# A recommendation tower on one Trainium2 core: the low half of a split product two operations behind, a tenth split step in every fourth unit, one tile turned later

## The chip, the cores and the metric

The kernel runs on one core of one Trainium2 chip. The metric is the device time of one launch in microseconds, the median of several runs. Five engines work side by side: TensorE (PE in the rows; its weight loads are PEld), VectorE (DVE), ScalarE (ACT), GpSimd (POOL) and SyncE (SP), which only issues transfers. They meet through semaphores.

## The reference

For each of 2048 rows, 39 embedding vectors of 16 numbers are looked up in 39 tables: `e[b, f, d]`. Two layers of crossed products follow, then a small dense tower:

```
z0 = einsum('bid,bjd->bdij', e, e)           # 39*39 products per (b, d)
cur0 = relu(z0 @ W0)                         # 128 channels
next_h, direct0 = split(cur0, 2)             # 64 go on, 64 go out
z1 = einsum('bid,bjd->bdij', e, next_h)      # 39*64 products per (b, d)
cur1 = relu(z1 @ W1)                         # 128 channels
z = sum over d of [direct0, cur1]            # 192 features
h = [z, dense_ctx]; two relu layers (512, 256) and a row of weights give y
```

Everything is in 32-bit floats. The time goes into the two einsums with their weights.

## The kernel before

**Tiles and units.** The batch is cut into 16 tiles of 128 rows, and each tile into two halves of the 16 embedding columns. That makes 32 units, numbered 0 to 31, of 1024 columns each (8 embedding columns times 128 rows). In a unit the products of one step stand on 128 partitions by 1024 columns, and the weights of the step (128 by 128) contract the partitions. The second layer has 20 steps in a unit, s0 to s19 (`step1`); s12 is a step on half the columns. The first layer of unit u+1 has 6 or 7 steps, here called a0 to a6 (`step0`), which are woven into unit u behind the steps named in `AFTER`. So a1 follows s1, a4 follows s7 and a5 follows s9.

**Whole and split steps.** VectorE multiplies two operands into a buffer (`make`, L965). A whole step goes into one of seven buffers `z`, and TensorE multiplies it in 32-bit floats (`product`, L561; each of its two matmuls shows as two records). A split step goes into one of three buffers `z_split`. ScalarE copies it to `z_hi` in the shorter type fp32r (`high`, L831), VectorE subtracts that from the product to get `z_lo` (`low`, L974), and TensorE makes three pairs of matmuls: `z_hi` with the high weights (L591), `z_hi` with the low weights (L594), `z_lo` with the high weights (L598, behind a wait on `z_lo_made`). In a unit the steps a1, a4 and s2, s3, s7, s8, s9, s13, s14 are split, nine in all, so VectorE has two operations for each of these and one for the others. In program order they stand in runs: a1, s2, s3, then s7, a4, s8, s9, then s13, s14.

**Who waits for what.** `make` of split number n waits until `z_lo` of split n-3 is made, since the `z_split` buffer is used again (L961). `high` of split n waits until TensorE has used split n-3 (L830). Each engine runs its instructions strictly in the order written. In what order VectorE makes its products and its `z_lo` is set by `low_before`, which is called behind each product; `place` is the number of a step in that order.

**Turning a tile.** GpSimd gathers the embedding rows of a tile (39 indirect DMAs, fewer for the first two tiles), TensorE transposes them (`turn_tile`, L553) at the step that `turn_step` names, ScalarE copies them out (`keep_tile`, L763 and L764) two steps later and issues four DMAs that store them (`store_tile`, L376), and SyncE loads the operands of the next tile's units from there. ScalarE stands in one row of work with this: in `body` the `keep_tile` comes ahead of the `high` of the same step. At the end of a unit ScalarE makes the operands of the next one from the first layer's result (`relu0`).

Of the kernel before, what the change touches and what calls it, by code (L numbers as in the profile page):

```python
# [35 lines left out]
STEPS1 = 2 + 2 * FQ  # L36
LAYS = 1 + FQ
SPLIT0 = (1, 4)
HALF1 = 12
SPLIT1 = (2, 3, 7, 8, 9, 13, 14)  # L40
WHOLE0 = tuple(s for s in range(STEPS0) if s not in SPLIT0)
REST0 = 3
EARLY = (2, 3)
WHOLE1 = tuple(s for s in range(STEPS1) if s not in SPLIT1 or s in EARLY)
ORDER0 = SPLIT0 + WHOLE0
AFTER = (0, 1, 3, 5, 7, 9, 11)
AHEAD = 2
# [51 lines left out]
def turn_step(u):  # L99

    if u % 2 or u + 2 >= UNITS:
        return None
    return {0: 11, 2: 7}.get(u, 2)


def lay_parts(n):
# [30 lines left out]
def at1(u, s):  # L137

    return FIRST1[u] + s + sum(a < s for a in after(u))
# [14 lines left out]

def split1(u):

    return tuple(s for s in SPLIT1 if u > 0 or s not in EARLY)


SPLIT_AT = sorted([at0(u, s) for u in range(UNITS) for s in split0(u)] + [at1(u, s) for u in range(UNITS) for s in split1(u)])  # L160
WHOLE_AT = sorted([at0(u, s) for u in range(UNITS) for s in range(steps0(u)) if s not in split0(u)] +
                  [at1(u, s) for u in range(UNITS) for s in range(STEPS1) if s not in split1(u)])
WHOLE_NO = {place: n for n, place in enumerate(WHOLE_AT)}
LEFT_AT = {at0(u, STEPS0 - 1): u for u in range(UNITS) if left_units(u)}
HALF_AT = {at1(u, HALF1) for u in range(UNITS)}
SPLIT_NO = {place: n for n, place in enumerate(SPLIT_AT)}


def shape_of(place):

    if place in LEFT_AT:
        return left_rows(LEFT_AT[place]), BANK
    return P, BANK if place in HALF_AT else C


def tower(nc, ids, tables, hot_ids, hot_tables, hot_consts, ident_in, dense_t, w0_a, w0_b, w1_whole, w1_split, top, top_small, y):
    ctx = ExitStack()
    with ctx:
        def sb(name, shape, dt=FP):
            return ctx.enter_context(nc.sbuf_tensor(name, shape, dt))  # L180
# [31 lines left out]
        w0_lo = sb("w0_lo", [P, len(SPLIT0), L], FR)  # L212
        w1 = sb("w1", [P, len(WHOLE1), L])
        w1_hi = sb("w1_hi", [P, len(SPLIT1), L], FR)
        w1_lo = sb("w1_lo", [P, len(SPLIT1), L], FR)
        small = sb("small", [P, K1 + K2 + K2])
# [22 lines left out]
        def half(t, u):  # L239
            return t[:, (u % 2) * C:(u % 2 + 1) * C]  # L240
# [30 lines left out]
        w0_raw_b = r0[:, C:C + STEPS0 * L].rearrange("p (s l) -> p s l", s=STEPS0)  # L271
        w1_raw = r1[:, 0:len(SPLIT1) * L].rearrange("p (s l) -> p s l", s=len(SPLIT1))

# [269 lines left out]
        def _(pe):  # L543
# [12 lines left out]
            def product(ps, place, k, w, first, last):  # L556

                pe.wait_ge(z_made, place + 1)
                for c in range(C // BANK):
                    cs = slice(c * BANK, (c + 1) * BANK)  # L560
                    mm = nc.tensor.matmul(ps[:, cs], w[0:k, :], z[WHOLE_NO[place] % NZ][0:k, cs], start=first, stop=last)  # L561
                mm.then_inc(z_used, 1)

            def half_product(ps, place, w, last):

                pe.wait_ge(z_made, place + 1)
                for n in range(2):
                    rows = slice(n * HROWS, (n + 1) * HROWS)
                    mm = nc.tensor.matmul(ps[:, n * BANK:(n + 1) * BANK], w[rows, :],  # L569
                                          z[WHOLE_NO[place] % NZ][rows, 0:BANK], start=False, stop=last)  # L570
                mm.then_inc(z_used, 1)
# [13 lines left out]
            def split_product(ps, place, k, w_hi, w_lo, first, last):  # L585

                n = SPLIT_NO[place]
                pe.wait_ge(z_hi_made, n + 1)
                for c in range(C // BANK):
                    cs = slice(c * BANK, (c + 1) * BANK)  # L590
                    nc.tensor.matmul(ps[:, cs], w_hi[0:k, :], z_hi[n % NS][0:k, cs], start=first, stop=False)  # L591
                for c in range(C // BANK):
                    cs = slice(c * BANK, (c + 1) * BANK)
                    nc.tensor.matmul(ps[:, cs], w_lo[0:k, :], z_hi[n % NS][0:k, cs], start=False, stop=False)  # L594
                pe.wait_ge(z_lo_made, n + 1)
                for c in range(C // BANK):
                    cs = slice(c * BANK, (c + 1) * BANK)
                    mm = nc.tensor.matmul(ps[:, cs], w_hi[0:k, :], z_lo[n % NS][0:k, cs], start=False, stop=last)  # L598
                mm.then_inc(z_used, 1)
# [14 lines left out]
            def step1(u, s):  # L614
                if s == 0 and u >= 2:
                    pe.wait_ge(relu1_done, u - 1)
                if s == HALF1:
                    half_product(half(psB, u), at1(u, s), w1[:, WHOLE1.index(s), :], False)
                elif s in split1(u):
                    n = SPLIT1.index(s)  # L620
                    split_product(half(psB, u), at1(u, s), P, w1_hi[:, n, :], w1_lo[:, n, :], s == 0, s == STEPS1 - 1)
                else:
                    product(half(psB, u), at1(u, s), P, w1[:, WHOLE1.index(s), :], s == 0, s == STEPS1 - 1)

# [57 lines left out]
            for u in range(UNITS):  # L682
                for s in range(STEPS1):
                    if s == turn_step(u):
                        turn_tile(u // 2 + 1)
                    step1(u, s)
                    if s in after(u):
                        step0(u + 1, after(u).index(s))
# [67 lines left out]
        def _(act):  # L756
# [76 lines left out]
            def body(u):  # L833
                for s in range(STEPS1):
                    if turn_step(u) is not None and s == turn_step(u) + 2:
                        keep_tile(u // 2 + 1)
                    if s in split1(u):
                        high(at1(u, s))
                    if s in after(u) and after(u).index(s) in split0(u + 1):
                        high(at0(u + 1, after(u).index(s)))  # L840
                    if s == REST0 and u == 0:
                        relu0_rest(0)
                    if s == 6 and u >= 1:
                        relu1(u - 1)
                    if s == 7 and u == UNITS - 1:
                        act.wait_ge(top_loaded, 32)
                        nc.scalar.activation(w_top_hi[:, 0:2 * C], w_top[0], ACT.Copy).then_inc(top_hi_made, 1)
                        nc.scalar.activation(w_top_hi[:, 2 * C:], w_top[1], ACT.Copy).then_inc(top_hi_made, 1)
                if u + 1 < UNITS:
                    relu0(u + 1)  # L850
# [101 lines left out]
        def _(dve):  # L952
# [14 lines left out]
            def low(place):  # L967

                k, cols = shape_of(place)
                n = SPLIT_NO[place]  # L970
                dve.wait_ge(z_hi_made, n + 1)
                if n >= NS:
                    dve.wait_ge(z_used, SPLIT_AT[n - NS] + 1)
                nc.vector.tensor_tensor(z_lo[n % NS][0:k, 0:cols], z_split[n % NS][0:k, 0:cols], z_hi[n % NS][0:k, 0:cols].bitcast(FP),  # L974
                                        ALU.subtract).then_inc(z_lo_made, 1)
# [47 lines left out]
                    relu_copy(h_quad[0][k][j * QUAD:(j + 1) * QUAD, BANK:C], rows, quad_copied)  # L1023

            def low_before(place):
                if place - 1 in SPLIT_NO:
                    low(place - 1)

            def sum0(q):
                dve.wait_ge(relu0_done, 4 * q + 4)  # L1030
# [27 lines left out]
            def body(u):  # L1058
                for s in range(STEPS1):
                    step1(u, s)  # L1060
                    if s == 17 and u == UNITS - 1:
                        split_top()
                    low_before(at1(u, s))
                    if u == 0 and s == 0:
                        copy_quad(0)
                    if s in after(u):
                        step0(u + 1, after(u).index(s))
                        low_before(at0(u + 1, after(u).index(s)))
                    if u == 0 and s == 1:
                        copy_quad(1)  # L1070
                    if s == 15 and u == 0:
                        dense_low()
                    if s == STEPS1 - 2 and u % 2 == 0 and u >= 2:
                        sum1(u // 2 - 1)
                    if s == STEPS1 - 2 and u % 4 == 3 and u < UNITS - 1:
                        sum0(u // 4)
# [119 lines left out]
            for s in range(STEPS0):  # L1196
                step0(0, s)
                low_before(at0(0, s))
# [144 lines left out]
```

## Time and profile before

| | |
|---|---|
| median of 3 runs | 1447.1 us (1446.37 to 1447.96) |
| the profiled execution | 1451.1 us, its span 1448.1 us |
| mean granted TensorE clock | 0.993 |
| TensorE busy | 1417.3 us (98% of the span) |
| VectorE busy | 1380.9 us (95%) |
| ScalarE busy | 783.7 us (54%) |
| GpSimd busy | 993.9 us (69%) |

The times in the trace count from the start of the span. The first products of unit 0 begin at 40.9 us, the steps of unit 31 end at about 1398 us, and the rest is the dense tower. A row of the timeline gives the start, the duration, the engine, the line, the operation with the tiles it writes and reads, and how many instructions are merged in it; in brackets stands the idle time ahead of it and who ended it. The time from one instruction's start to the next one's on the same engine tells what it costs there; durations overlap a little.

### The profile page before, as it was taken

The numbers are of one execution on the slowest core, as the hardware profiler recorded it, in microseconds if no ns is written. First come the engines' busy times: TensorE is split into PE (matmuls) and PEld (weight loads), VectorE is DVE, ScalarE is ACT, GpSimd is POOL, SyncE is SP. The second block draws the span as 40 slices with busy tenths as digits, with TensorE's granted clock in tenths as the row PEclk, the third lists the DMA queues.
The fourth block names the chain that finished last, engine by engine and source line by source line (L and its number), as shares of the span: only waits on it lengthen the run. The fifth ranks groups of instructions, "written<-read, shape, count | busy, mean of one in ns | idle before, by whom it ended". The sixth has DMA issues, their size and how long they took to land.

```text
span 1448.1 us, 14670 instructions
## 1 busy us (share of the span) xinstructions
PE 1417.3 (98%) x4408; PEld 783.3 (54%) x4408; DVE 1380.9 (95%) x1243; ACT 783.7 (54%) x833; POOL 993.9 (69%) x604
## 2 busy tenths in 40 slices
PE   4999999999999999999999999999999999999999
PEld 3545554555555555555555555555555555555556
DVE  6899999999999999999999999999999999999983
ACT  1555446555455656545465565545656554565655
POOL 7888888888888888888888888888888840000000
PEclk7999999999999999999999999999999999999999
DMA  5979788788888888878788887888898877777600
GB/s 156 212 190 236 185 223 200 196 219 201 203 210 200 215 205 217 213 197 216 205 200 211 213 225 190 205 210 206 203 224 212 211 201 198 201 200 208 180 13 0
DMA packets 130779, 282.64 MB, mean 195 GB/s; under 512 B 36532, under 2 KB 61764, under 8 KB 130572
## 3 DMA queue, kind: packets, MB, share of 16 engines
q1 hardware_dynamic: 96588, 268.31, 70.6%
q0 software_dynamic: 19200, 4.95, 4.1%
q10 hardware_dynamic: 14912, 8.46, 2.0%
q8 instruction: 34, 0.56, 0.2%
q14 instruction: 45, 0.37, 0.1%
HBM read 273.67 MB, written 7.87 MB: 194 GB/s over the span
## 4 chain that ended last, share of the span: by engine, by line
PE 81%; POOL 13%; issue 3%; DVE 1%; DMA 1%; ACT 0%; DVEq 0%; POOLq 0%
PE psB L561 39%; POOL emb L538 13%; PE psA L561 13%; PE psB L591 6%; PE psB L594 6%; PE psB L598 6%; PE psB L569 2%; PE psA L591 2%; PE psA L594 2%; PE psA L598 2%; PE psA L581 1%; PE psB L693 1%; PE psA L553 1%; PE psB L695 1%; PE psB L694 1%
## 5 line engine op out<-in xcount | busy, mean ns | idle before, releaser
L538 POOL DMA_INDIRECT emb<-in_tbl,ids_all x600 | 993.7, 1656 | 185.0 <-issue 182.6
L561 PE MATMUL psB<-z,w 128*128 128x512 f32 x1544 | 689.3, 592 | 2.6 <-DVE z L965 2.6
L831 ACT ACTIVATE z_hi<-z_split 128x1024 fp32r<-128x1024 f32 x285 | 301.0, 1060 | 512.2 <-DVE z_split L965 447.2
L561 PEld LDWEIGHTS psB<-z,w 128*128 128x128 f32 x1544 | 292.7, 190 | 358.2 <-issue 333.5
L965 DVE TENSOR_TENSOR z<-h_quad,x_lay 128x1024 f32<-128x1024 f32 x354 | 419.0, 1213 | 2.0 <-issue 1.3
L974 DVE TENSOR_TENSOR z_lo<-z_split,z_hi 128x1024 fp32r<-128x1024 f32 x285 | 348.9, 1224 | 21.0 <-ACT z_hi L831 20.9
L965 DVE TENSOR_TENSOR z_split<-h_quad,x_lay 128x1024 f32<-128x1024 f32 x222 | 266.6, 1213 | 0.0
L785 ACT ACTIVATE h_quad<-psA 32x1024 f32<-32x1024 f32 x248 | 251.8, 1015 | 6.7 <-DVE feat_side L1056 3.1
L561 PE MATMUL psA<-z,w 128*128 128x512 f32 x516 | 242.2, 592 | 0.5 <-DVE z L965 0.5
L591 PE MATMUL psB<-z_hi,w_hi 128*128 128x512 f32 x444 | 155.9, 432 | 0.0
L561 PEld LDWEIGHTS psA<-z,w 128*128 128x128 f32 x516 | 97.4, 189 | 99.5 <-issue 91.0
L598 PE MATMUL psB<-z_lo,w_hi 128*128 128x512 f32 x444 | 138.6, 393 | 1.7 <-DVE z_lo L974 1.6
L594 PE MATMUL psB<-z_hi,w_lo 128*128 128x512 f32 x444 | 138.6, 394 | 0.0
L965 DVE TENSOR_TENSOR z<-bases,x_more 128x1024 f32<-128x1024 f32 x93 | 112.7, 1212 | 0.4 <-DMA x_more<-x_tiles 0.4
L591 PEld LDWEIGHTS psB<-z_hi,w_hi 128*128 128x128 f32 x444 | 80.1, 189 | 52.1 <-issue 37.6
L598 PEld LDWEIGHTS psB<-z_lo,w_hi 128*128 128x128 f32 x444 | 82.8, 189 | 23.5 <-DVE z_lo L974 5.8
L594 PEld LDWEIGHTS psB<-z_hi,w_lo 128*128 128x128 f32 x444 | 83.7, 188 | 18.7
L777 ACT ACTIVATE h_pair<-psA 64x1024 f32<-64x1024 f32 x62 | 62.9, 1015 | 5.7 <-PE psA L581 5.1
L822 ACT ACTIVATE r<-psB 128x1024 f32<-128x1024 f32 x32 | 33.1, 1035 | 41.5 <-PE psB L598 25.1
L591 PE MATMUL psA<-z_hi,w_hi 128*128 128x512 f32 x126 | 52.0, 493 | 0.3 <-ACT z_hi L831 0.3
L965 DVE TENSOR_TENSOR z<-bases,x_ring 128x1024 f32<-128x1024 f32 x32 | 38.8, 1212 | 0.8 <-DMA bases<-x_tiles 0.8
L594 PE MATMUL psA<-z_hi,w_lo 128*128 128x512 f32 x126 | 39.2, 393 | 0.0
(126 smaller groups left out, 757.7 us busy)
## 6 DMA issues: line engine op xcount, KB each, us to landing
x_lay<-x_tiles SPq DMA_DIRECT2D x1152, 128.0 KB
bases<-x_tiles SPq DMA_DIRECT2D x62, 468.0 KB
x_more<-x_tiles SPq DMA_DIRECT2D x62, 468.0 KB
x_lay<-x_tiles SPq DMA_DIRECT2D x64, 256.0 KB
x_ring<-x_tiles SPq DMA_DIRECT2D x31, 468.0 KB
emb<-in_tbl,ids_all POOLq DMA_INDIRECT x600
x_last<-x_tiles SPq DMA_DIRECT2D x64, 128.0 KB, 9.7
x_tiles<-x_side ACTq DMA_DIRECT2D x14, 256.0 KB
```

Of the source, the lines that this page charges most:

```text
L538: nc.gpsimd.indirect_dma_start(emb[t % 2][:, f * D:(f + 1) * D], None, tables[f], bass.IndirectOffsetOnAxis(ids_all[:, t, f:f + 1], 0)).th ...
L561: mm = nc.tensor.matmul(ps[:, cs], w[0:k, :], z[WHOLE_NO[place] % NZ][0:k, cs], start=first, stop=last)
L569: mm = nc.tensor.matmul(ps[:, n * BANK:(n + 1) * BANK], w[rows, :], z[WHOLE_NO[place] % NZ][rows, 0:BANK], start=False, stop=last)
L591: nc.tensor.matmul(ps[:, cs], w_hi[0:k, :], z_hi[n % NS][0:k, cs], start=first, stop=False)
L594: nc.tensor.matmul(ps[:, cs], w_lo[0:k, :], z_hi[n % NS][0:k, cs], start=False, stop=False)
L598: mm = nc.tensor.matmul(ps[:, cs], w_hi[0:k, :], z_lo[n % NS][0:k, cs], start=False, stop=last)
L777: op = nc.scalar.activation(h_pair[n * H:(n + 1) * H, :], h[0:H, :], ACT.Relu)
L785: op = nc.scalar.activation(h_quad[u % 2][k][n * QUAD:(n + 1) * QUAD, :], h[k * QUAD:(k + 1) * QUAD, :], ACT.Relu)
L822: nc.scalar.activation(r1_by_b[:, :, u % 2 * DH:(u % 2 + 1) * DH], by_d, ACT.Relu).then_inc(relu1_done, 1)
L831: nc.scalar.activation(z_hi[n % NS][0:k, 0:cols], z_split[n % NS][0:k, 0:cols], ACT.Copy).then_inc(z_hi_made, 1)
L965: nc.vector.tensor_tensor(out[0:k, 0:cols], a[0:k, 0:cols], b[0:k, 0:cols], ALU.mult).then_inc(z_made, 1)
L974: nc.vector.tensor_tensor(z_lo[n % NS][0:k, 0:cols], z_split[n % NS][0:k, 0:cols], z_hi[n % NS][0:k, 0:cols].bitcast(FP), ALU.subtract).th ...
```

## The change

Three edits. `low_before(place)` now makes the `z_lo` of the product two places back, where it was one place back. Step s5 becomes a split step in the units 1, 5, 9, ..., 29 (`u % 4 == 1`, eight of them), so these have ten split steps; the other units keep s5 whole, and the weights of s5 are held in both forms. The turn of tile 3 (the fourth), which is made in unit 4, stands ahead of s5 instead of s2, and with it its `keep_tile` on ScalarE moves from ahead of s4 to ahead of the `high` of s7.

```
-SPLIT1 = (2, 3, 7, 8, 9, 13, 14)
+SPLIT1 = (2, 3, 5, 7, 8, 9, 13, 14)
+TENTH = 5
...
-WHOLE1 = tuple(s for s in range(STEPS1) if s not in SPLIT1 or s in EARLY)
+WHOLE1 = tuple(s for s in range(STEPS1) if s not in SPLIT1 or s in EARLY + (TENTH,))
...
-    return {0: 11, 2: 7}.get(u, 2)
+    return {0: 11, 2: 7, 4: 5}.get(u, 2)
...
-    return tuple(s for s in SPLIT1 if u > 0 or s not in EARLY)
+    return tuple(s for s in SPLIT1 if (u > 0 or s not in EARLY) and (u % 4 == 1 or s != TENTH))
...
             def low_before(place):
-                if place - 1 in SPLIT_NO:
-                    low(place - 1)
+                if place - 2 in SPLIT_NO:
+                    low(place - 2)
```

On VectorE in unit 17, the products of s7, a4, s8 and s9 and their `z_lo` stand so in the program before; the numbers behind the names are those of the buffers.

```order
L965 TENSOR_TENSOR z_split2<-h_quad1_0,x_lay 128x1024
L965 TENSOR_TENSOR z_split0<-bases,x_more 128x1024
L974 TENSOR_TENSOR z_lo2<-z_split2,z_hi2 128x1024
L965 TENSOR_TENSOR z_split1<-h_quad1_1,x_lay 128x1024
L974 TENSOR_TENSOR z_lo0<-z_split0,z_hi0 128x1024
L965 TENSOR_TENSOR z_split2<-h_quad1_0,x_lay 128x1024
L974 TENSOR_TENSOR z_lo1<-z_split1,z_hi1 128x1024
L965 TENSOR_TENSOR z6<-bases,x_more 128x1024
L974 TENSOR_TENSOR z_lo2<-z_split2,z_hi2 128x1024
```

The same place in the changed program, where a line added above shifts the line numbers by one:

```order
L966 TENSOR_TENSOR z_split1<-h_quad1_0,x_lay 128x1024
L966 TENSOR_TENSOR z_split2<-bases,x_more 128x1024
L966 TENSOR_TENSOR z_split0<-h_quad1_1,x_lay 128x1024
L975 TENSOR_TENSOR z_lo1<-z_split1,z_hi1 128x1024
L966 TENSOR_TENSOR z_split1<-h_quad1_0,x_lay 128x1024
L975 TENSOR_TENSOR z_lo2<-z_split2,z_hi2 128x1024
L966 TENSOR_TENSOR z1<-bases,x_more 128x1024
L975 TENSOR_TENSOR z_lo0<-z_split0,z_hi0 128x1024
L966 TENSOR_TENSOR z2<-h_quad1_1,x_lay 128x1024
L975 TENSOR_TENSOR z_lo1<-z_split1,z_hi1 128x1024
```

Each `z_lo` stands one operation later, and the fourth product of the run (the second `z_split1`) now stands directly behind the `z_lo1` that frees its buffer, where two operations lay between such a pair (`z_lo2` and the second `z_split2`) before.

On VectorE a little ahead of that in unit 17, from the `z_lo` of s3 to the product of s7, before:

```order
L974 TENSOR_TENSOR z_lo1<-z_split1,z_hi1 128x1024
L965 TENSOR_TENSOR z2<-h_quad1_1,x_lay 128x1024
L965 TENSOR_TENSOR z3<-h_quad1_0,x_lay 128x1024
L965 TENSOR_TENSOR z4<-bases,x_more 128x1024
L965 TENSOR_TENSOR z5<-h_quad1_1,x_lay 128x1024
L965 TENSOR_TENSOR z_split2<-h_quad1_0,x_lay 128x1024
```

The same stretch in the changed program, from the `z_lo` of s3, which has the product of s4 ahead of it now, to the product of s7:

```order
L975 TENSOR_TENSOR z_lo2<-z_split2,z_hi2 128x1024
L966 TENSOR_TENSOR z_split0<-h_quad1_0,x_lay 128x1024
L966 TENSOR_TENSOR z6<-bases,x_more 128x1024
L966 TENSOR_TENSOR z0<-h_quad1_1,x_lay 128x1024
L975 TENSOR_TENSOR z_lo0<-z_split0,z_hi0 128x1024
L966 TENSOR_TENSOR z_split1<-h_quad1_0,x_lay 128x1024
```

The product of s5 goes into a `z_split` buffer (`z_split0`), and its `z_lo0`, an operation that the program before does not have, stands ahead of the run of s7.

On ScalarE in unit 4 the program before has the copies of tile 3 and its four DMAs ahead of the copy `r` and of the six `z_hi` of the unit's second part:

```order
L831 ACTIVATE z_hi<-z_split 128x1024 x3
L763 ACTIVATE x_side<-psA 128x512
L764 ACTIVATE x_side<-psA 112x128
L376 DMA x_tiles<-x_side 128x4x128
L376 DMA x_tiles<-x_side 112x128
L376 DMA x_tiles<-x_side 128x2x128
L376 DMA x_tiles<-x_side 80x128
L822 ACTIVATE r<-psB 128x128x8
L831 ACTIVATE z_hi<-z_split 128x1024 x6
```

And in the changed program:

```order
L832 ACTIVATE z_hi<-z_split 128x1024 x3
L823 ACTIVATE r<-psB 128x128x8
L764 ACTIVATE x_side<-psA 128x512
L765 ACTIVATE x_side<-psA 112x128
L377 DMA x_tiles<-x_side 128x4x128
L377 DMA x_tiles<-x_side 112x128
L377 DMA x_tiles<-x_side 128x2x128
L377 DMA x_tiles<-x_side 80x128
L832 ACTIVATE z_hi<-z_split 128x1024 x6
```

The copies and the DMAs of the tile now stand directly ahead of the `z_hi` of s7.

## Rows read from the trace of the kernel before

**Rows 1.** The page, part 1: busy us, share of the span, instructions.
```profile
PE 1417.3 (98%) x4408; PEld 783.3 (54%) x4408; DVE 1380.9 (95%) x1243; ACT 783.7 (54%) x833; POOL 993.9 (69%) x604
```
**Rows 2.** VectorE's waits from 280 to 1390 us: total, times, longest.
```profile
DVE z_lo L974 <- ACT z_hi L831: 12.1, 14, 1.4
```
**Rows 3.** ScalarE in order of time, unit 18, s9.
```profile
842.50 1.07 ACT L831 ACTIVATE z_hi<-z_split 128x1024 fp32r<-128x1024 f32 x1 [2.79 <-PE psB L598]
```
**Rows 4.** VectorE in order of time, units 18, 20 and 21, around s9.
```profile
843.60 1.23 DVE L974 TENSOR_TENSOR z_lo<-z_split,z_hi 128x1024 fp32r<-128x1024 f32 x1 [0.44 <-ACT z_hi L831]
...
927.67 1.21 DVE L974 TENSOR_TENSOR z_lo<-z_split,z_hi 128x1024 fp32r<-128x1024 f32 x1
...
961.33 1.21 DVE L965 TENSOR_TENSOR z_split<-bases,x_more 128x1024 f32<-128x1024 f32 x1
962.54 1.25 DVE L974 TENSOR_TENSOR z_lo<-z_split,z_hi 128x1024 fp32r<-128x1024 f32 x1
...
968.26 1.21 DVE L965 TENSOR_TENSOR z<-bases,x_more 128x1024 f32<-128x1024 f32 x1
969.39 1.21 DVE L974 TENSOR_TENSOR z_lo<-z_split,z_hi 128x1024 fp32r<-128x1024 f32 x1
```
**Rows 5.** TensorE in order of time, units 18, 20 and 21, s9.
```profile
845.88 0.62 PE L598 MATMUL psB<-z_lo,w_hi 128*128 128x512 f32 x2
...
929.70 0.62 PE L598 MATMUL psB<-z_lo,w_hi 128*128 128x512 f32 x2
...
970.75 0.64 PE L598 MATMUL psB<-z_lo,w_hi 128*128 128x512 f32 x2
```
**Rows 6.** TensorE in order of time, unit 17, ahead of s7 and behind s9.
```profile
796.38 1.88 PE L561 MATMUL psB<-z,w 128*128 128x512 f32 x4
...
803.63 1.88 PE L561 MATMUL psA<-z,w 128*128 128x512 f32 x4
```
**Rows 7.** TensorE in order of time, unit 4 (first five) and unit 18.
```profile
236.20 1.03 PE L591 MATMUL psA<-z_hi,w_hi 128*128 128x512 f32 x2
...
240.59 0.76 PE L553 MATMUL psA<-ident,emb 128*128 128x128 f32 x5 [2.46 <-DMA emb<-in_tbl,ids_all]
...
245.53 1.88 PE L561 MATMUL psA<-z,w 128*128 128x512 f32 x4
247.25 3.60 PE L561 MATMUL psB<-z,w 128*128 128x512 f32 x8
...
259.15 0.62 PE L598 MATMUL psB<-z_lo,w_hi 128*128 128x512 f32 x2
...
827.18 1.03 PE L591 MATMUL psA<-z_hi,w_hi 128*128 128x512 f32 x2
...
832.27 1.02 PE L561 MATMUL psA<-z,w 128*128 128x512 f32 x2
```
**Rows 8.** VectorE in order of time, before unit 0 and in unit 1.
```profile
37.60 1.22 DVE L1194 COPY x_lay<-psB 128x1024 f32<-128x1024 f32 x1
38.85 1.22 DVE L965 TENSOR_TENSOR z<-x_lay 128x1024 f32<-128x1024 f32 x1
...
103.89 1.23 DVE L965 TENSOR_TENSOR z_split<-bases,x_ring 128x1024 f32<-128x1024 f32 x1 [1.09 <-DMA bases<-x_tiles]
...
125.81 1.21 DVE L974 TENSOR_TENSOR z_lo<-z_split,z_hi 128x1024 fp32r<-128x1024 f32 x1
```
**Rows 9.** TensorE in order of time, unit 1, s9.
```profile
127.08 0.73 PE L598 MATMUL psB<-z_lo,w_hi 128*128 128x512 f32 x2 [0.51 <-DVE z_lo L974]
```
**Rows 10.** Two stretches: engines' busy us and instructions, granted clock, DMA share, GB/s.
```profile
62.00:70.00 8.00, 6.32 (x16) 2.55 (x15) 6.13 (x7) 2.88 (x5) 6.17 (x7) 1.00 0.99 225
...
241.60:245.60 4.00, 4.00 (x12) 3.11 (x12) 4.00 (x5) 1.50 (x4) 3.60 (x2) 0.57 0.93 269
```
**Rows 11.** ScalarE in order of time, unit 2, around the turn of tile 2.
```profile
165.05 0.60 ACT L763 ACTIVATE x_side<-psA 128x512 f32<-128x512 f32 x1 [1.35 <-PE psA L553]
...
167.93 1.06 ACT L831 ACTIVATE z_hi<-z_split 128x1024 fp32r<-128x1024 f32 x1 [2.12 <-PE psA L598]
```

## The prediction

> **What bounds the kernel now.** I read the busy shares first, then the waits by engine, then the timelines of TensorE and VectorE side by side. The page shows two engines almost full, TensorE at 98% and VectorE at 95% [rows 1], so shares alone don't say which one sets the end. The waits do: from 280 to 1390 us VectorE waits 12.1 us in all, 14 times, always for `z_hi` [rows 2], and TensorE has no wait there. VectorE runs ahead of TensorE and is stopped now and then. The stop can be read in unit 18: `z_hi` of s9 begins when TensorE has used the split product three before it [rows 3], and `z_lo` of s9 waits for that [rows 4].
>
> What counts for this change is how far ahead. I take the time from the end of `z_lo` of s9 to the start of the matmul that reads it, and call it the reserve; s9 is where it is smallest in a unit, since in the run s7, a4, s8, s9 each `z_lo` comes 2.27 us after the last (two operations), while TensorE needs less per product. Unit 18: 843.60 + 1.23 = 844.83, read at 845.88, reserve 1.05. Unit 20: 929.70 - 928.88 = 0.82. Unit 21: 970.75 - 970.60 = 0.15 [rows 4, 5]. The pattern returns every four units: the stop in units 18, 22, ... leaves 1.05, and by units 21, 25, ... it is eaten down to 0.15. So VectorE's spare time exists, but it is lost at the stop, and units 5, 9, ..., 29, which get the tenth split step, are those with the least reserve.
>
> **The change part by part.**
>
> *The tenth split step on TensorE.* From the whole product ahead of s7 to the one behind s9 is 803.63 - 796.38 = 7.25 us [rows 6]. A whole product costs 247.25 - 245.53 = 1.72 [rows 7], so four split products cost 5.53, or 1.38 each. Each new split step gives TensorE 0.34 us. Eight of them make 2.7 us.
>
> *On VectorE* it is one operation more. From 968.26 to 969.39 is 1.13 us [rows 4]; I take 1.14.
>
> *z_lo two behind.* It takes away a small wait at the head of each of the three runs in a unit: from 961.33 to 962.54 is 1.21 [rows 4], 0.07 over the pitch, so 0.21 a unit. It adds one: the fourth product of the run now stands directly behind the `z_lo` whose end it needs. How much such a wait costs is bounded by 0 and by the nearest pair, a copy and the product that reads it: 38.85 - 37.60 = 1.25 [rows 8], 0.12 over the pitch. I take 0.12, since it is the same kind of wait on the engine's own result. Net gain on VectorE 0.09 a unit. The page "VectorE: DVE Perf Modes" of the Trainium skill, section "The DRAIN you can't avoid", says that a semaphore between operations of this engine costs nothing. By that the sum below would be 2.5 us less, 1451.0; the pair in the trace speaks for 0.12.
>
> The later place itself neither gives nor takes reserve once VectorE has been stopped: the stop is at a `z_lo`, which now has one more product ahead of it, and every later `z_lo` has that same product ahead of it too. Only before the first stop is the place paid for.
>
> *Unit 1.* There VectorE is held at 103.89 by a load and has no reserve at s9: TensorE waits for its `z_lo`, which starts at 125.81 [rows 8, 9]. Behind that load it now has one operation more (1.14), `z_lo` one place later (1.14), 0.12 for the new wait, less 0.21: +2.2 us. In units 2 and 3 I count nothing: in unit 2 VectorE is stopped again, and the rest moves with TensorE.
>
> *The turn of tile 3.* TensorE stands 2.46 us for the last gather, and then runs at a granted clock of 0.57 [rows 7, 10], part of it at the lower of its two levels (1.2 GHz). From a1 to a2 it takes 245.53 - 236.20 = 9.33; the same stretch with a turn and no wait, in unit 18, 832.27 - 827.18 = 5.09 [rows 7]. So 4.25 us go. At s5 the turn would start at 247.25 + 1.72 - 4.25 - 0.59 (the turn itself, no longer ahead of it; 0.5 to 0.7 by its five transposes) + 2.2 = 246.3, which is 5.7 us behind the landing at 240.59.
>
> But ScalarE now copies and stores the tile directly ahead of `z_hi` of s7. In unit 2 that takes from 165.05 to the end of the next `z_hi` at 168.99, 3.94 us [rows 11]. In unit 4 `z_hi` of s7 so ends at 246.3 + 0.76 + 3.94 = 251.0. Behind it on VectorE wait, in order, `z_lo` of s7, s9's product, `z_lo` of a4, a5's product, `z_lo` of s8, s10's product and `z_lo` of s9: its start is 251.0 + 6 x 1.14 + 0.12 = 258.0 and its end 259.2. TensorE read it at 259.15 before [rows 7]. So by s9 of unit 4 the 4.25 us are used up: 2.2 by unit 1, the rest by this. Level there: +0.1 us.
>
> *Unit 5.* It starts from no reserve (0.05 is what a matmul that waited shows). Unit 20 to 21 costs 0.82 - 0.15 = 0.67; the new operation 1.14 and TensorE's own gain 0.34 also come off, 0.09 comes back: 0.05 - 0.67 - 1.14 - 0.34 + 0.09 = -2.01. TensorE waits 2.06 at s8 and s9, less 0.34 gained: +1.7.
>
> *Units 9, 13, ..., 29.* From the stop three units earlier: 0.15 - 1.14 - 0.34 + 3 x 0.09 = -1.06, a wait of 1.1, less 0.34: +0.77 each, +4.6 for six.
>
> *At nothing:* the larger split weights at the start (128 columns more on ScalarE and VectorE, and their load) lie ahead of the gathers of tile 0 that the first products wait for; without that cover, a few tenths. The other tiles' loads: their stores end about as late in their unit as those of tile 2.
>
> *Sum:* 0.1 + 1.7 + 4.6 = +6.4. The profiled execution took 1451.1 us, of which 1448.1 is the span; it would become 1457.5. The median of the runs is 4.0 below the profiled one, so 1447.1 + 6.4 = **1453.5 us**.
>
> **The rivals.**
>
> *A, TensorE alone decides* (faster). If VectorE always has the operands ready, only TensorE's terms count: -2.7 - 4.25 = -7.0, 1440.1. For it: 98% busy and no waits of TensorE behind 280 us. Against: the reserve of 0.15 where 1.14 is put in. It decides if the reserve at s9 of unit 21 is over 1.5.
>
> *B, the later place buys reach* (no change). If the extra product ahead of each stop does lift the reserve behind it by a full operation, 1.14, units 9 to 29 wait no longer and give 0.34 each: 0.1 + 1.7 - 2.0 = -0.2, 1446.9. For it: 14 stops, all at `z_lo` [rows 2]. Against: the reading `z_lo` is later by the same step.
>
> *C, the clock falls in the new waits* (slower). After the 2.46 us wait the 4 us at 0.57 [rows 10] cost 4.25 - 2.46 = 1.8 us. If that followed each of the seven waits, 7 x 1.8 = 12.6: 1466. If only that of unit 5: 1455.3. Against: from 62 to 70 us TensorE is busy only 6.32 of 8 us, and the clock stays 1.00 [rows 10]. The Trainium skill ("TensorE: Matmul & The Clock Gate", section "What's actually happening") says that the low clock is the state of an idle array and activity lifts it; the trace agrees, by the 0.57 behind the wait.
>
> *D, ScalarE does not hold unit 4* (little change). If `z_hi` of s7 is there in time, unit 4 keeps 4.25 - 2.2 = 2.05, and unit 5 starts with some 0.5 more and waits 1.55: -2.05 + 1.2 + 4.6 = +3.8, 1450.9. With half the later waits, 1448.6.
>
> **How the numbers follow.** Forecast 0.60 (its own range 1450 to 1457: the new wait between 0 and 0.2, unit 1 by one operation more or less); C 0.06; D with smaller waits, and B, together 0.16; A 0.18. The range takes in B and part of A below, and one fall of the clock above: 1443 to 1459. A measurement tells 0.2% (2.9 us) from no change: faster is below 1444.2, slower above 1450.0. Faster 0.19 (A and a little of B), same 0.12, slower 0.69.
>
> **What would show it.** Right: in units 9, 13, ..., 29 the third pair of matmuls of s8 and s9 waits for `z_lo`, about 1.1 us in all, and 2 us in unit 5; VectorE still waits for `z_hi` in units 6, 10, ...; in unit 4 no wait for the gather, a clock of 1.00, and `z_hi` of s7 behind the four DMAs. The forecast is wrong if TensorE shows no waits for `z_lo` behind 260 us, or if s9's reserve in unit 21 is positive.

## The result, and the profile after

The changed kernel takes **1466.8 us** (median of 4 runs, 1466.55 to 1468.84), against 1446.7 us for the kernel before on the same chip: 1.0135 times as long, 95% interval 1.0123 to 1.0147. The direction was forecast, the size was not: 20 us more against 6.4. The time lies above the range. The profiled execution took 1467.0 us, 15.9 us more than the profiled one before, with a span of 1465.1 us, 17.0 us more. The profiled execution of before lay 4 us above its median and this one does not, so the rows of before hold some 4 us that most of its executions do not have; where these lie is not shown.

The page tells little: 1420.1 us of TensorE (1417.3 before), 1385.2 of VectorE (1380.9) [rows 1].

```profile
PE 1420.1 (97%) x4424; PEld 785.4 (54%) x4424; DVE 1385.2 (95%) x1251; ACT 787.9 (54%) x841; POOL 1011.9 (69%) x604
```

Where the 17 us lie is read best unit by unit: the start of the first matmul of s0 in a unit, to that of the next unit.

| stretch | before | after | difference | forecast |
|---|---|---|---|---|
| up to s0 of unit 0 | 56.10 | 56.83 | +0.7 | 0 |
| unit 0 | 46.92 | 55.10 | **+8.2** | **0** |
| unit 1 | 43.46 | 45.41 | +1.95 | +2.2 |
| unit 2 | 42.13 | 42.16 | 0 | 0 |
| unit 3 | 42.84 | 45.60 | **+2.8** | **0** |
| unit 4 | 45.89 | 44.41 | -1.5 | -2.1 |
| unit 5 | 42.17 | 43.87 | +1.7 | +1.7 |
| units 9, 13, ..., 29 | 42.15 to 42.21 | 42.93 to 43.00 | +4.7 in all | +4.6 |
| all other units | 41.05, 41.64 or 42.17 | the same | 0 | 0 |
| from s0 of unit 31 to the end | 81.78 | 80.18 | -1.6 | 0 |

In the last row, TensorE of the kernel before waited 1.06 us for `feat_side` at the start of the dense tower, and 0.30 us for a `z_lo` of unit 31; in the changed kernel neither wait is there. The four kernels measured with `z_lo` one behind up to the end take 81.8 to 82.6 us in this stretch, the ten with two behind 80.2 to 81.5.

**The new waits where they were forecast.** TensorE in unit 21, from the first pair of s8 over the third pairs of s8 and of s9 to the product behind them [answers rows 5]:

```profile
984.33 0.62 PE L592 MATMUL psB<-z_hi,w_hi 128*128 128x512 f32 x2
...
985.42 0.73 PE L599 MATMUL psB<-z_lo,w_hi 128*128 128x512 f32 x2
...
987.69 0.73 PE L599 MATMUL psB<-z_lo,w_hi 128*128 128x512 f32 x2 [0.61 <-DVE z_lo L975]
988.26 1.88 PE L562 MATMUL psA<-z,w 128*128 128x512 f32 x4
```

The same stretch before:

```profile
968.49 0.62 PE L591 MATMUL psB<-z_hi,w_hi 128*128 128x512 f32 x2
...
971.23 1.88 PE L561 MATMUL psA<-z,w 128*128 128x512 f32 x4
```

It takes 988.26 - 984.33 = 3.93 us, against 971.23 - 968.49 = 2.74: the two waits cost 1.19 us, where about 1.1 was forecast. The 0.61 in brackets is only the engine's idle time ahead of the second.

VectorE behind it, in the same unit [answers rows 4]:

```profile
979.38 1.22 DVE L975 TENSOR_TENSOR z_lo<-z_split,z_hi 128x1024 fp32r<-128x1024 f32 x1
980.70 1.23 DVE L966 TENSOR_TENSOR z_split<-h_quad,x_lay 128x1024 f32<-128x1024 f32 x1
...
986.42 1.21 DVE L975 TENSOR_TENSOR z_lo<-z_split,z_hi 128x1024 fp32r<-128x1024 f32 x1
```

`z_lo` of s9 ends at 986.42 + 1.21 = 987.63 and is read at 987.69: the reserve of 0.15 has become the 0.06 of a matmul that waited. The first two rows are the wait on the engine's own result: 980.70 - 979.38 = 1.32, 0.18 over the pitch of 1.14, where I took 0.12. The 30 such pairs of this trace start 1.31 to 1.33 us apart.

VectorE's own stops for `z_hi` from 280 to 1390 us fell from 12.1 us to 8.4 [answers rows 2]:

```profile
DVE z_lo L975 <- ACT z_hi L832: 8.4, 13, 0.9
```

**Unit 4**, ScalarE and then TensorE [answers rows 7]:

```profile
258.53 0.60 ACT L764 ACTIVATE x_side<-psA 128x512 f32<-128x512 f32 x1 [9.15 <-PE psA L554]
259.02 0.27 ACT L765 ACTIVATE x_side<-psA 112x128 f32<-112x128 f32 x1
259.32 2.42 ACTq L377 DMA_DIRECT2D x_tiles<-x_side  x4
261.84 2.96 ACT L832 ACTIVATE z_hi<-z_split 128x1024 fp32r<-128x1024 f32 x3 [2.55 <-issue]
```

```profile
257.78 0.71 PE L554 MATMUL psA<-ident,emb 128*128 128x128 f32 x5
...
266.68 0.73 PE L599 MATMUL psA<-z_lo,w_hi 128*128 128x512 f32 x2 [0.72 <-DVE z_lo L975]
...
268.95 0.72 PE L599 MATMUL psB<-z_lo,w_hi 128*128 128x512 f32 x2 [0.61 <-DVE z_lo L975]
...
271.22 0.73 PE L599 MATMUL psB<-z_lo,w_hi 128*128 128x512 f32 x2 [0.62 <-DVE z_lo L975]
```

The turn waits for no gather, the granted clock is 1.00 from 256 to 276 us, `z_hi` of s7 stands behind the four DMAs, and TensorE pays 0.72 + 0.61 + 0.62 = 1.95 us for it at a4, s8 and s9.

**What was not forecast** stands in the chain of work that ended last, among its longest pieces (start, us, what):

```profile
76.07 12.25 POOL emb L539
...
192.57 11.19 DMA x_lay<-x_tiles
```

*Unit 0.* One gather of tile 1 took 12.25 us. GpSimd in order of time:

```profile
73.80 1.96 POOL L539 DMA_INDIRECT emb<-in_tbl,ids_all  x1 [0.30 <-issue]
76.07 12.25 POOL L539 DMA_INDIRECT emb<-in_tbl,ids_all  x1 [0.30 <-issue]
88.62 0.94 POOL L539 DMA_INDIRECT emb<-in_tbl,ids_all  x1 [0.30 <-issue]
```

VectorE at the same time; between 66.9 and 87.5 us it has no pause:

```profile
73.73 1.22 DVE L966 TENSOR_TENSOR z_split<-h_quad,x_lay 128x1024 f32<-128x1024 f32 x1
...
86.29 1.21 DVE L966 TENSOR_TENSOR z<-h_quad,x_lay 128x1024 f32<-128x1024 f32 x1
96.72 1.22 DVE L975 TENSOR_TENSOR z_lo<-z_split,z_hi 128x1024 fp32r<-128x1024 f32 x1 [9.22 <-ACT z_hi L832]
```

The gather ended at 76.07 + 12.25 = 88.32, that is 0.82 us after VectorE's last operation (86.29 + 1.21 = 87.50). The gather ahead of it, at 73.80, met the operation of 73.73 and ended at 75.76, also 0.81 after that one's end (74.95). With VectorE idle, as at 88.62, a gather takes 0.94. The kernel before has a pause at this place: with one behind, a `z_lo` waits there for its `z_hi`. VectorE and then GpSimd, before:

```profile
75.06 0.67 DVE L965 TENSOR_TENSOR z<-left_a,left_b 50x512 f32<-50x512 f32 x1
76.27 1.23 DVE L974 TENSOR_TENSOR z_lo<-z_split,z_hi 128x1024 fp32r<-128x1024 f32 x1 [0.53 <-ACT z_hi L831]
```

```profile
75.13 1.44 POOL L538 DMA_INDIRECT emb<-in_tbl,ids_all  x1 [0.31 <-issue]
```

With two behind that `z_lo` comes later and finds its `z_hi` made. In the changed kernel TensorE stands for the tile, and then runs slow:

```profile
93.62 1.33 PE L554 MATMUL psA<-ident,emb 128*128 128x128 f32 x5 [7.34 <-DMA emb<-in_tbl,ids_all]
```

In the two windows around that stand the granted clock falls from 1.00 (TensorE busy 1.88 of 4.00 us) to 0.61 (busy 2.38 of 7.60), part of the time on the lower of its two levels (1.2 of 2.4 GHz):

```profile
84.40:88.40 4.00, 1.88 (x5) 0.56 (x3) 3.10 (x3) 0.00 (x0) 3.92 (x1) 1.00 0.00 0
88.40:96.00 7.60, 2.38 (x7) 1.80 (x8) 0.00 (x0) 1.02 (x3) 5.66 (x6) 0.61 0.07 7
```

The Trainium skill ("SBUF — State Buffer", section "Who interferes with whom") says that a `tensor_tensor` with both inputs in SBUF contends with GpSimd's reads of SBUF, and marks as inferred that it does not hold up the writing of DMA descriptors, since it takes only the read side of the port pair that the two engines share. The trace shows the gather, which reads its row numbers (`ids_all`) from SBUF, slowed: 0.94 us with VectorE idle, 1.96 beside `tensor_tensor`, and once 12.25. Whether the reading or the descriptors waited it does not tell.

*Unit 3.* VectorE's product of s3 waits 2.81 us for a load:

```profile
199.75 1.22 DVE L966 TENSOR_TENSOR z_split<-h_quad,x_lay 128x1024 f32<-128x1024 f32 x1
203.78 1.23 DVE L966 TENSOR_TENSOR z_split<-h_quad,x_lay 128x1024 f32<-128x1024 f32 x1 [2.81 <-DMA x_lay<-x_tiles]
204.93 1.22 DVE L975 TENSOR_TENSOR z_lo<-z_split,z_hi 128x1024 fp32r<-128x1024 f32 x1
```

With two behind, that product stands ahead of `z_lo` of a1 (204.93), s2 and s3, and TensorE waits for all three (206.20 [0.46], 208.47 [0.62], 210.74 [0.60]):

```profile
206.20 0.73 PE L599 MATMUL psA<-z_lo,w_hi 128*128 128x512 f32 x2 [0.46 <-DVE z_lo L975]
...
208.47 0.74 PE L599 MATMUL psB<-z_lo,w_hi 128*128 128x512 f32 x2 [0.62 <-DVE z_lo L975]
...
210.74 0.73 PE L599 MATMUL psB<-z_lo,w_hi 128*128 128x512 f32 x2 [0.60 <-DVE z_lo L975]
```

### The profile page after: what moved, and what is told of

Read it like the earlier page. It is cut to its first block, busy times and chain, and to the rows that moved or that the text cites. A ratio compares the mean times of both kernels' runs of the same rounds, so it can differ in the third digit from the quotient of the medians.

```text
span 1465.1 us, 14734 instructions
## 1 busy us (share of the span) xinstructions
PE 1420.1 (97%) x4424; PEld 785.4 (54%) x4424; DVE 1385.2 (95%) x1251; ACT 787.9 (54%) x841; POOL 1011.9 (69%) x604
## 4 chain that ended last, share of the span: by engine, by line
PE 87%; POOL 5%; issue 3%; DVE 3%; DMA 1%; ACT 0%; SPq 0%; DVEq 0%; ACTq 0%; POOLq 0%
PE psB L562 42%; PE psA L562 14%; PE psB L599 7%; PE psB L592 7%; PE psB L595 6%; POOL emb L539 5%; PE psB L570 2%; PE psA L592 2%; PE psA L595 2%; PE psA L599 2%; DVE z_lo L975 2%; PE psA L582 1%; DMA x_lay<-x_tiles 1%; PE psA L554 1%; PE psB L694 1%
## 5 line engine op out<-in xcount | busy, mean ns | idle before, releaser
L539 POOL DMA_INDIRECT emb<-in_tbl,ids_all x600 | 1011.7, 1686 | 185.0 <-issue 182.5
L562 PE MATMUL psB<-z,w 128*128 128x512 f32 x1512 | 676.4, 593 | 1.1 <-DVE z L966 1.1
L832 ACT ACTIVATE z_hi<-z_split 128x1024 fp32r<-128x1024 f32 x293 | 306.3, 1058 | 469.6 <-DVE z_split L966 345.2
L562 PEld LDWEIGHTS psB<-z,w 128*128 128x128 f32 x1512 | 287.3, 190 | 348.4 <-issue 322.1
L975 DVE TENSOR_TENSOR z_lo<-z_split,z_hi 128x1024 fp32r<-128x1024 f32 x293 | 356.5, 1217 | 20.9 <-ACT z_hi L832 20.8
L966 DVE TENSOR_TENSOR z_split<-h_quad,x_lay 128x1024 f32<-128x1024 f32 x230 | 275.3, 1219 | 10.5 <-DMA x_lay<-x_tiles 5.3
L592 PE MATMUL psB<-z_hi,w_hi 128*128 128x512 f32 x460 | 163.7, 437 | 0.0
L599 PE MATMUL psB<-z_lo,w_hi 128*128 128x512 f32 x460 | 144.9, 396 | 11.6 <-DVE z_lo L975 11.3
L562 PEld LDWEIGHTS psA<-z,w 128*128 128x128 f32 x516 | 97.3, 189 | 96.0 <-issue 87.5
L764 ACT ACTIVATE x_side<-psA 128x512 f32<-128x512 f32 x16 | 9.6, 599 | 77.5 <-PE psA L554 77.5
L599 PE MATMUL psA<-z_lo,w_hi 128*128 128x512 f32 x126 | 39.4, 394 | 2.6 <-DVE z_lo L975 2.6
```

The costliest lines, as they stand in the source:

```text
L539: nc.gpsimd.indirect_dma_start(emb[t % 2][:, f * D:(f + 1) * D], None, tables[f], bass.IndirectOffsetOnAxis(ids_all[:, t, f:f + 1], 0)).th ...
L832: nc.scalar.activation(z_hi[n % NS][0:k, 0:cols], z_split[n % NS][0:k, 0:cols], ACT.Copy).then_inc(z_hi_made, 1)
L966: nc.vector.tensor_tensor(out[0:k, 0:cols], a[0:k, 0:cols], b[0:k, 0:cols], ALU.mult).then_inc(z_made, 1)
```

## The experiments

Ratios are to the kernel before, run on the same chip. The profile of each was read in the same way.

**1. Only `z_lo` two behind** (the kernel before, with `place - 2` in `low_before`).

> Only z_lo two operations behind; splits and turn as before. Theory 1 (the start: without the little pauses that z_lo one behind gave VectorE in unit 0, a gather of tile 1 is held on GpSimd until VectorE stops): unit 0 is longer by about 8 us again, one gather of tile 1 takes over 10 us, and unit 3 pays some 2 to 3 us for a load of x_lay that the earlier product waits for: 1446.7 + 8 + 2.5 + 1 = about 1458. Theory 2 (the larger split weights and their load at the start delay the gathers): they are not here, so unit 0 is as before and the time is 1447 to 1450.

Measured: 1458.4 us, ratio 1.0067 (1.0046 to 1.0088). Unit 0 takes 56.95 us, unit 3 45.61 (VectorE waits 2.8 us for the load). GpSimd, and VectorE's last operation ahead of its pause:

```profile
75.22 12.25 POOL L538 DMA_INDIRECT emb<-in_tbl,ids_all  x1 [0.30 <-issue]
```

```profile
85.44 1.21 DVE L965 TENSOR_TENSOR z<-h_quad,x_lay 128x1024 f32<-128x1024 f32 x1
```

75.22 + 12.25 = 87.47, 0.82 after 86.65. Theory 2 falls. Unit 4 here takes 41.65 us with the turn where it was: TensorE comes 14.5 us later and the gather of tile 3 is there. The units 5 to 30 are as before, so two behind in itself neither costs nor gains there; it lifts the reserve of s9 in unit 21 from 0.15 to 0.50 us, and the stretch from s0 of unit 31 is 1.6 us shorter, as in the changed kernel.

**2. Only the tenth split step** (`SPLIT1`, `TENTH`, `WHOLE1`, `split1` as in the change; `place - 1`, turn at s2).

> Only the tenth split step in units 1, 5, ..., 29; z_lo one behind and the turn as before. Theory 1: unit 0 as before, no gather over 4 us; the seven later units wait 0.09 to 0.3 us longer each than in the changed kernel, since three little waits per unit stay: about 1 us each, and 1 to 2 us in unit 1: 1446.7 + 7 + 1.5 = about 1455. Theory 2: unit 0 is longer by 8 us here too: about 1463.

Measured: 1455.3 us, ratio 1.0045 (1.0030 to 1.0060). Unit 0 takes 45.89 us, so the larger weights delay nothing. Units 9, 13, ..., 25 take 43.41 to 43.45, 1.25 us more than before. With two behind it was 0.8, so the later place saves these units 0.45 us each.

**3. Only the turn at s5** (`{0: 11, 2: 7, 4: 5}`).

> Only the turn of tile 3 at s5. Both theories: unit 0 as before. The stand of 2.46 us for the gather and the low clock behind it go (4.25 us), and ScalarE's keep_tile ahead of z_hi of s7 gives back some 2 us or more in units 4 and 5: 1446.7 - 2 = about 1444.7. If ScalarE did not hold the unit: 1442.5.

Measured: 1448.8 us, ratio 1.0008 (0.9995 to 1.0021): no gain, where 1444.7 or 1442.5 was expected. Unit 4 falls by 2.0 us, and unit 5 takes 0.65 more. Units 2 and 3 take 1.4 more, where VectorE waits 2.0 us for two loads of `x_lay`, and unit 0 takes 1.0 less. But up to unit 4 this program and the one before run the same instructions, so these are differences between two executions and not the work of the turn; unit 4 begins at 232.43 us, against 231.45 before. The three edits alone come to 0.67 + 0.45 + 0.08 = 1.2%, together 1.35%.

**4. The change, with one behind in unit 0.**

```
+            def lag(p):
+                return 1 if p < at1(0, 19) else 2
             def low_before(place):
-                if place - 2 in SPLIT_NO:
-                    low(place - 2)
+                for p in (place - 2, place - 1):
+                    if p in SPLIT_NO and p + lag(p) == place:
+                        low(p)
```

> The changed kernel, with z_lo one behind up to s19 of unit 0 and two behind from there. Theory 1: the gathers of tile 1 take under 4 us each, unit 0 falls back by 8 us, all later units as in the changed kernel: 1466.8 - 8.2 = about 1458.6. Theory 2: no change, 1466 to 1467.

Measured: 1457.2 us, ratio 1.0063 (1.0043 to 1.0083). Unit 0 takes 46.16 us, no gather is held; units 4 to 30 are as in the changed kernel. So the place of `z_lo` in unit 0 alone costs some 9 us. In all ten kernels measured with one behind in unit 0 it takes 44.77 to 46.92 us, in the three with two behind and no pause put in 55.10 to 56.95.

**5. The change, with one pause of VectorE in unit 0.**

```
             def make(place, a, b):
+                if place == at1(0, 10):
+                    dve.wait_ge(z_used, at1(0, 7) + 1)
```

> The changed kernel with one wait more on VectorE: in unit 0 the product of s10 waits until TensorE has used the product of s7, a pause of some 1.6 us at about 79 us, in the middle of the gather that took 12.25 us. Theory 1 (the gather of tile 1 cannot go on while VectorE works without a pause): it ends about 0.8 us after the pause begins, so it takes some 3.7 us (76.1 to 79.8), the turn of tile 1 waits under 2 us for the last gather, and the pause itself costs TensorE at most 1.3 us: 1466.8 - 8.2 + 1.3 = about 1460, 1458 to 1461. Rival (the 12.25 us are the gather's own, a fixed time or something in its queue): it takes 12 us again and the time is 1467 or more.

Measured: 1459.3 us, ratio 1.0076 (1.0059 to 1.0092): a wait put in saves 7 us, 5.0 of them in unit 0 (50.13 us). VectorE and GpSimd:

```profile
77.18 1.21 DVE L968 TENSOR_TENSOR z_split<-h_quad,x_lay 128x1024 f32<-128x1024 f32 x1
80.06 1.23 DVE L968 TENSOR_TENSOR z<-h_quad,x_lay 128x1024 f32<-128x1024 f32 x1 [1.68 <-PE psB L599]
```

```profile
75.51 3.70 POOL L539 DMA_INDIRECT emb<-in_tbl,ids_all  x1 [0.30 <-issue]
79.52 0.94 POOL L539 DMA_INDIRECT emb<-in_tbl,ids_all  x1 [0.30 <-issue]
```

The pause begins at 77.18 + 1.21 = 78.39, the gather ends at 79.21, 0.82 later. The hold is no time of the gather's own.

**6. The change, with one operation of VectorE cut short.**

```
+                if place == at0(1, STEPS0 - 1):
+                    cols -= 64
```

> The changed kernel with one operation of VectorE cut short: the product of the left-over rows in unit 0 (z<-left_a,left_b 50x512, just ahead of the gather that took 12.25 us) makes 448 of its 512 columns, which leaves 64 columns of that product unmade. VectorE still has no pause there, but each of its operations from there on starts some 0.07 us sooner. Theory 1a (a gather is held where the VectorE operation that runs at its issue ends 0.602 to 0.611 us after the issue, as with all nine held ones in ten traces; an end at 0.53 lets it through): the gather takes about 1.36 us, the turn of tile 1 waits under 1 us, unit 0 falls by 7 to 8 us: about 1459. Theory 1b (any gather issued in a stretch where VectorE has no pause can be held, whatever the offset): 12 us again and 1466 to 1467.

Measured: 1468.4 us, ratio 1.0144 (1.0127 to 1.0161). The operation that ran at the gather's issue now ended 0.54 us behind it, and the gather was held all the same:

```profile
76.40 12.19 POOL L539 DMA_INDIRECT emb<-in_tbl,ids_all  x1 [0.30 <-issue]
```

```profile
86.55 1.21 DVE L968 TENSOR_TENSOR z<-h_quad,x_lay 128x1024 f32<-128x1024 f32 x1
```

76.40 + 12.19 = 88.59, again 0.83 after 87.76. My theory 1a, an offset of 0.602 to 0.611 us, falls. What picks the gather that is held stays open: in later units VectorE runs 42 us and more without a pause, and behind unit 0 no gather of any of the traces takes more than 2.02 us.

**7. The turn of tile 2 at s3** (kernel 4 with `{0: 11, 2: 3, 4: 5}`).

> The kernel with z_lo one behind in unit 0, with the turn of tile 2 (in unit 2) at s3 and not at s7. Theory 1 (in unit 3 the product of s3 waits 2.4 us for a load of x_lay that stands on SyncE behind the store of tile 2, and the three z_lo behind it make TensorE wait): the store ends about 10 us earlier, the wait of that product and TensorE's waits for z_lo of a1, s2, s3 in unit 3 go, unit 3 takes 42.2 to 42.9 and not 45.1: 1457.2 - 2.2 = about 1455. Rival (the load waits for its buffer, or for the queue's own length, not for the store): unit 3 stays at 45 and the time at 1457.

Measured: 1457.7 us, ratio 1.0075 (1.0056 to 1.0094). Unit 3 takes 42.18 us (45.08 in kernel 4), and VectorE has no wait at s2 and s3:

```profile
192.04 2.35 DVE L966 TENSOR_TENSOR z_split<-h_quad,x_lay 128x1024 f32<-128x1024 f32 x2
```

SyncE issues the load from 178.45 us on, against 181.72 in kernel 4: 3.3 us sooner, more than the 2.33 us that the product waited there. So the load behind the store is the cause in unit 3, though unit 3 also begins 2.1 us later here, which alone would have covered most of the wait. The time is not won: unit 2 takes 1.6 us more, since the turn now comes too soon for its own gather, and unit 1 (0.7 us) and the stretch from unit 31 on (0.9 us), which the edit does not touch, take more as well:

```profile
158.54 0.77 PE L554 MATMUL psA<-ident,emb 128*128 128x128 f32 x5 [1.90 <-DMA emb<-in_tbl,ids_all]
```

**8. The tenth step in units 2, 6, ..., 30** (kernel 4 with `u % 4 == 2`).

> The kernel with z_lo one behind in unit 0, with the tenth split step in units 2, 6, ..., 30 and not 1, 5, ..., 29. Theory 1 (each unit of four has VectorE stopped for some 1.7 to 2.1 us at two z_lo of units 6, 10, ..., so an operation more there comes out of the stop; in units 5, 9, ... there is nothing to take it from): units 9, 13, ... fall from 43.0 to about 42.3, units 6, 10, ... from 41.64 to 41.3: about 1.0 us for each four units, 6 to 7 us in all, and 1 to 2 us more from units 1 and 5: 1457.2 - 8 = about 1449. Rival (one operation more per four units costs the same wherever it stands): 1456 to 1458.

Measured: 1461.6 us, ratio 1.0094 (1.0077 to 1.0111). Both theories missed it: it is dearer there. Even units turn a tile at s2, and ScalarE copies and stores it ahead of s5's `z_hi` (unit 18), for which VectorE stands:

```profile
837.67 0.60 ACT L764 ACTIVATE x_side<-psA 128x512 f32<-128x512 f32 x1 [4.22 <-PE psA L554]
...
838.47 2.39 ACTq L377 DMA_DIRECT2D x_tiles<-x_side  x4
840.96 1.06 ACT L832 ACTIVATE z_hi<-z_split 128x1024 fp32r<-128x1024 f32 x1 [2.52 <-DVE z L966]
```

```profile
842.04 1.23 DVE L975 TENSOR_TENSOR z_lo<-z_split,z_hi 128x1024 fp32r<-128x1024 f32 x1 [1.28 <-ACT z_hi L832]
```

**9. Everything mended** (one behind up to s19 of unit 3, the tenth step in units 6, 10, ..., 30, the turn of tile 3 at s4, and in unit 4 `relu1` at s10).

> Meant to beat both: z_lo one behind in units 0 to 3 and two behind from there, the tenth split step in units 6, 10, ..., 30, the turn of tile 3 at s4 with the copy r of that unit moved on ScalarE behind z_hi of s9. Theory 1: 1446.7 - 7 x 0.34 (tenth step, out of VectorE's stops) - about 2.5 (no stand for the gather, with a smaller hold by ScalarE) = about 1442, 1440 to 1444. Rival (unit 4 gives back all and the tenth step takes the reserve of units 9, 13, ...): 1446 to 1448.

Measured: 1458.6 us, ratio 1.0072 (1.0055 to 1.0090). Both forecasts missed, for the reason of experiment 8; unit 4 itself falls to 43.22 us. TensorE's waits from 290 us on:

```profile
PE psB L599 <- DVE z_lo L975: 8.0, 20, 0.6
```

**10. The same, with `keep_tile` of those units two steps later.**

```
-                    if turn_step(u) is not None and s == turn_step(u) + 2:
+                    if turn_step(u) is not None and s == turn_step(u) + (4 if u % 4 == 2 and u > 2 else 2):
```

> The kernel with all three mended, with keep_tile of units 6, 10, ..., 30 on ScalarE two steps later, behind z_hi of the tenth step s5. Theory 1 (there the tenth step was slow since keep_tile and its four DMAs stood ahead of its z_hi, and VectorE stood 1.2 us for it): that stand goes, units 6, 10, ... take 41.3 and units 7, 11, ... 42.2 to 42.4: 1458.5 - 6 x 1.5 = about 1449, and 1444 if the hold does not come back at z_hi of s7. Rival (one VectorE operation more is 1.14 us, wherever it stands, and the stops are no spare time): no change, 1457 to 1459.

Measured: 1449.3 us, ratio 1.0008 (0.9997 to 1.0019): 9 us come back, so `keep_tile` was the cause in 9, and in 8 by the same rows. TensorE's and VectorE's waits from 290 us on:

```profile
PE psB L599 <- DVE z_lo L975: 2.5, 9, 0.4
```

```profile
DVE z_lo L975 <- ACT z_hi L832: 5.1, 6, 0.9
```

Units 10, 14, 18 and 22 take 41.4 us (41.64 before), units 26 and 30 take 0.1 and 0.3 us more than before, and units 11, 15, ... 42.7 (42.17). So the step is still no gain: of VectorE's stops only those at s9 could be spent; the six of 0.9 us at a1, ahead of the step, remain.

**11, 12. Only the turn at s4, with `relu1` of unit 4 at s10; and the same with two behind from the end of unit 3 on.**

```
-    return {0: 11, 2: 7}.get(u, 2)
+    return {0: 11, 2: 7, 4: 4}.get(u, 2)
...
-                    if s == 6 and u >= 1:
+                    if s == (10 if u == 4 else 6) and u >= 1:
```

> The kernel before with one thing changed in unit 4: the turn of tile 3 stands at s4, and on ScalarE the copy r of that unit stands behind z_hi of s9. z_lo one behind and nine split steps everywhere. Theory 1 (the stand of 2.46 us and the low clock go, and with s4 and r out of the way ScalarE gives z_hi of s7 some 3.5 us sooner than with s5): unit 4 falls from 45.9 to about 43, less 0.5 us given back in unit 5: 1446.7 - 2.5 = about 1444. Rival (what the turn gains is given back through the loads of x_lay in units 2 and 3 and through units 5 and 6, as with s5 alone): 1446 to 1449.

> The same with z_lo two behind from the end of unit 3 on. Theory 1 (two behind gives VectorE 0.09 us a unit, which raises the reserve of units 9, 13, ... from 0.1 to 0.5 us but shortens nothing, since TensorE sets the pace there): the same time as with one behind, within 1 us, about 1443 to 1444; units 5 and up take 42.17 and 41.64. Rival (the later place costs in itself): 1447 or more.

Measured: 1448.3 us, ratio 1.0004 (0.9995 to 1.0012), and 1446.5 us, ratio 0.9991 (0.9983 to 1.0000). The times that theory 1 gave, about 1444 and 1443 to 1444, are missed by some 3 to 4 us. Unit 4 falls to 43.24 and 43.08 us, as expected, and unit 5 takes 0.5 to 0.6 more in both. In the first, units 2 and 3 take 1.9 us more (VectorE waits 2.7 us for two loads of `x_lay`) and unit 0 takes 2.1 less, again with the same instructions as before up to unit 4. In the second, units 8 and 9 take 0.5 us more each, and the stretch from s0 of unit 31 is 1.6 us shorter than in the first. The second is the only kernel below the kernel before, by 1.4 us, with an interval that ends at no change. That the stand of 2.46 us is met in every execution of the kernel before isn't shown: its one profile lies 4 us above its median.

## Why the prediction fell short

- **What bounds it**, reserve and stops: right, but for one wait of TensorE, 0.30 us in unit 31, where I read none. Units 9 to 29 pay 0.74 to 0.84 us against 0.77, unit 5 1.70 against 1.7, unit 1 1.95 against 2.2. Rival A (TensorE alone) falls by these waits.
- **The later place gives no reach** (rival B's denial): right; two behind lifts the reserve of unit 21 to 0.50 us (experiment 1), not by a full operation of 1.14, and units 9 to 29 wait in the changed kernel.
- **The wait on VectorE's own result**: 0.18, not 0.12. Two behind still gains VectorE more than I took: the reserve of unit 21 rose by 0.35 us over the three units behind the stop, 0.12 a unit and not 0.09.
- **Unit 4**: right in its mechanism, 0.6 us too hopeful. Rival D (ScalarE does not hold it) falls by the 3.21 us for which VectorE stood for that `z_hi`.
- **Rival C** (the clock): it names nearly the time that came out, but not the cause. In the new waits of units 5 and 21 the clock stays at 1.00 (TensorE busy 7.38 and 7.37 of 8 us); it fell behind the stand of 7.34 us, which I had not foreseen:

```profile
304.00:312.00 8.00, 7.38 (x25) 4.36 (x24) 7.90 (x8) 3.77 (x4) 6.48 (x6) 1.00 0.67 175
984.00:992.00 8.00, 7.37 (x24) 4.06 (x23) 8.00 (x9) 1.12 (x2) 6.78 (x5) 1.00 0.91 228
```

- **The step that failed is *z_lo two behind*.** I priced the later place on VectorE alone: a small wait taken away at the head of each run, 0.09 us gained a unit, and otherwise nothing but what unit 1 pays. The sum has no term for unit 0; at the start I asked only what the change adds, the larger split weights, and these do cost nothing (experiment 2). What it takes away there is the pause in which a gather of GpSimd came through. Without it the gather is held for 12.25 us, TensorE stands 7.34 us for the tile, and unit 0 takes 8.2 us more (experiments 1, 4 and 5). The chain of work on the page of before had named GpSimd, and I did not ask why:

```profile
PE 81%; POOL 13%; issue 3%; DVE 1%; DMA 1%; ACT 0%; DVEq 0%; POOLq 0%
```

- **"In units 2 and 3 I count nothing" failed too, by 2.8 us.** I followed what stands behind a moved `z_lo`, but not the operation that now stands ahead of it: the product of s3 and its load (experiment 7). How much of the 2.8 is due to the change is not settled. Experiments 3 and 11, which run the instructions of the kernel before up to unit 4, took 43.66 and 43.89 us in unit 3, with a wait of 0.75 and 0.99 us for such a load; the six kernels with two behind and the turn of tile 2 at s7 took 43.40 to 45.61, with a wait of 0.68 to 2.81.

Without these two, 17.0 - 8.2 - 2.8 = +6.0 us are left on the span, against the forecast of +6.4. That they lie so close is in part luck: the forecast terms came to 1.95 - 1.5 + 1.7 + 4.7 = +6.9, and the +0.7 ahead of unit 0 and the -1.6 at the end were not forecast.

## What to carry to other kernels

When an operation is moved back in an engine's order, list what now stands ahead of it, with the loads that this waits for, and ask who else lived on the pause that it leaves. Where GpSimd gathers are on the chain, a pause of the vector engine is not waste: here one wait put in saved 7 us. Spare time counts only where it stands: of VectorE's stops the ones ahead of the new step could not pay for it, and a copy on ScalarE stood in the way of the rest.

## What the runs showed of the hardware

- A GpSimd gather takes 0.94 us with VectorE idle. Issued just behind the start of a two-input VectorE operation it takes 1.96 to 1.98, and ends 0.81 to 0.82 us after that operation's end.
- Now and then one is held through the whole row of VectorE operations, and ends 0.82 to 0.83 us after the next pause begins: 12.25, 12.25, 12.19 and 3.70 us in the four kernels with two behind in unit 0. Shorter holds, 2.56 to 3.70 us, stand at 47 to 49 us in ten of the fourteen traces, the kernel before among them (48.24, 2.57 us). So a hold comes with either place of `z_lo`; how long it lasts goes by VectorE's next pause.
- A VectorE operation that waits for the result of the one directly ahead of it starts 1.31 to 1.33 us after it (30 pairs in the changed kernel), 0.18 over the pitch of 1.14.
